# The first layer's experts computed for two chosen experts per token, in 39 gathered tiles, instead of for all eight

## The reference, cut to what matters

```python
xn = _layernorm(x)
x = x + _L0_attn_ref(xn, wq, wk, wv, wa, wg, wo, rms_scale) + _L0_ffn_ref(xn, wqkv, w1, w2)

# attention: a complex gate, a scan over the 512 tokens of a sequence
a_c = sigmoid(|a|) * exp(i * angle(a));  y = q * real(scan(a_c, k * v));  return (y * silu(g)) @ wo

# experts: E = 8, F = 352, the best TOP_K = 2 of a token
top_logits, idx = lax.top_k(logits, 2);  scores = softmax(top_logits)
for e in range(8):
    a, g = split(x_rep @ w1[e].T)              # 128 -> 2 * 352
    he = silu(a) * g @ w2[e].T                 # 352 -> 128
    out = out + where(expert_ids == e, he, 0)
out = (out * scores).reshape(N, 2, h).sum(axis=1)
```

## Time and profile before

| | us |
|---|---|
| median of 3 runs | 523.91 (523.36 to 526.57) |
| profiled execution | 524.22 |
| its span, first to last instruction | 522.4 |
| head, until the first attention matmul | 44.3 |
| each of the first three turns of the loop | 64.5 |
| fourth turn, until the last 12 token tiles' statistics begin | 59.9 (237.8 to 297.7) |
| until the first normalised token tile of layer two (L895) | 304.92 |
| second layer | 217.5 |

### The profile page before, as it was taken

How to read it: one execution, slowest core, us unless ns; L and a number is a source line. 1 busy time by engine, 2 the same in 40 slices (tenths; PEclk the granted TensorE clock), 3 DMA queues, 4 the chain that set the end, 5 groups by cost and what they waited for, 6 DMA issues and landing times.

```text
span 522.4 us, 7319 instructions
## 1 busy us (share of the span) xinstructions
PE 442.2 (85%) x2143; PEld 325.9 (62%) x2143; DVE 382.8 (73%) x702; ACT 278.1 (53%) x392; POOL 194.8 (37%) x188
## 2 busy tenths in 40 slices
PE   2729999999999999999989969299689778977893
PEld 1327887888878888788877845155455445544452
DVE  5687478944888448894498987776768877887784
ACT  2375674426644275533655255835676577557730
POOL 1248014400144001530002100740477778777850
PEclk9958999999999999999999979579799999999997
DMA  6420001100012000000000000000265776687664
GB/s 177 96 61 23 2 0 43 43 1 0 0 41 52 0 0 0 0 0 0 1 0 2 1 0 1 0 2 0 55 130 114 144 141 131 116 157 137 126 130 120
DMA packets 29535, 26.76 MB, mean 51 GB/s; under 512 B 10837, under 2 KB 25414, under 8 KB 29510
## 3 DMA queue, kind: packets, MB, share of 16 engines
q0 software_dynamic: 4608, 16.78, 16.8%
q1 hardware_dynamic: 24902, 9.69, 7.3%
HBM read 8.64 MB, written 1.05 MB: 19 GB/s over the span
## 4 chain that ended last, share of the span: by engine, by line
PE 29%; DVE 28%; POOL 19%; issue 13%; ACT 7%; DMA 2%; DVEq 1%; SPq 0%; POOLq 0%; ACTq 0%
POOL state L435 9%; PE psum L1083 7%; PE psum L203 6%; PE psum L205 6%; PE psum L204 6%; POOL xn_tok L439 4%; POOL g_hi L448 3%; DVE hid L771 2%; PE psum L1203 2%; DVE at_m L800 1%; DVE at_m L802 1%; POOL g_lo L449 1%; DVE xn_tok L693 1%; POOL sel_now L450 1%; PE psum L1218 1%
## 5 line engine op out<-in xcount | busy, mean ns | idle before, releaser
L567 ACT ACTIVATE sil<-psum 128x512 f32<-128x512 f32 (+1 forms) x96 | 56.3, 596 | 104.3 <-PE psum L205 91.2
L771 DVE TENSOR_TENSOR hid<-sil,psum 128x512 f32<-128x512 f32 (+1 forms) x96 | 65.1, 686 | 51.8 <-PE psum L205 32.9
L1083 PEld LDWEIGHTS psum<-e_w,hid 128*128 128x128 f32 (+1 forms) x768 | 94.9, 191 | 6.0
L1083 PE MATMUL psum<-e_w,hid 128*128 128x128 f32 (+1 forms) x768 | 95.3, 274 | 0.0
L203 PE MATMUL psum<-xn_hi,e_hi 128*128 128x512 f32 (+1 forms) x192 | 81.8, 426 | 7.9 <-DVE hid L771 7.3
L975 DVE TENSOR_TENSOR_SCAN state<-dec,win_t 128x1024 f32<-128x1024 f32 x32 | 73.4, 2295 | 20.0 <-ACT dec L643 20.0
L205 PE MATMUL psum<-xn_lo,e_hi 128*128 128x512 f32 (+1 forms) x192 | 76.0, 396 | 0.0
L204 PE MATMUL psum<-xn_hi,e_lo 128*128 128x512 f32 (+1 forms) x192 | 75.8, 395 | 0.0
L652 ACT ACTIVATE sil<-psum,vec_t 128x512 f32<-128x512 f32 x64 | 43.2, 687 | 47.3 <-PE psum L205 36.8
L435 POOL TENSOR_SCALAR state<-state,ssm_cb 128x1024 f32<-128x1024 f32 x32 | 49.7, 1552 | 45.2 <-DVE state L975 42.2
L1258 PE MATMUL psum<-hid,g_w 128*128 128x512 f32 x128 | 61.3, 592 | 0.0
(11 more groups left out here) (261 smaller groups left out, 766.5 us busy)
## 6 DMA issues: line engine op xcount, KB each, us to landing
xn_tok<-state POOLq DMA_DIRECT2D x32, 512.0 KB, 4.5
e_raw<-in_L_ffn_w SPq DMA_DIRECT2D x16, 128.0 KB, 2.1
e_raw<-in_L_ffn_w SPq DMA_DIRECT2D x8, 176.0 KB, 2.4
res<-in_L_attn_x SPq DMA_DIRECT2D x4, 256.0 KB, 3.9
g_raw<-in_L_ffn_w SPq DMA_DIRECT2D x16, 64.0 KB, 2.3
g_w<-in_L_ffn_w SPq DMA_DIRECT2D x16, 64.0 KB, 2.5
out<-res SPq DMA_DIRECT2D x4, 256.0 KB, 2.9
e_raw<-in_L_ffn_w SPq DMA_DIRECT2D x16, 48.0 KB, 1.9
```

What stands on the lines that cost most here:

```text
L567: act.activation(sil[0:M, s % 2, :], ps[s % 2][0:M, :], ACT.Silu).then_inc(silu_done, 1)
L771: dve.tensor_tensor(hid[0:M, tb % 2, ft, :], sil[0:M, s % 2, :], ps[2 + s % 2][0:M, :], ALU.mult).then_inc(gated, 1)
L1083: ins = pe.matmul(ps[4 + o % 2][:, n * P:(n + 1) * P], hid[0:m, tb % 2, ft, n * P:(n + 1) * P], e_w2[j][0:m, ft, :], start=(ft == 0), stop ...
```

## The change

**What it does.** All eight experts' weights are turned, copied and split before the first layer's main part, and stay in SBUF (`w_hi`, `w_lo`, `w_out`). After the mask `chosen`, PE counts with two matmuls how many tokens chose each expert, and some thirty small DVE instructions give every (token, choice) pair a slot in a table of 39 tiles of 128 slots, each tile of one expert; 39 is the 32 tiles that 4096 pairs fill, plus 7 for rounding up. SP fills the table `slots` in HBM with zeros; POOL writes the 2048 tokens twice to it, by 32 indirect DMAs of 128 rows. A row is 130 numbers: the token, its weight, its place in the output.

**Tiles.** SP loads a tile of slots (`x_tile`, a ring of six); from the seventh on it waits until the output of the tile six before has landed. Per tile PE turns it (`turn_x`), makes 2 x 352 hidden channels with six matmuls (`hidden`), turns them (`turn_hidden`) and multiplies with w2 (`output`). The number of the tile's expert is read by PE from SBUF into a register (`value_load`), for `hidden` and again for `output`. ACT copies, applies Silu, copies and weighs (`copy_x`, `tile_silu`, `copy_hidden`, `weigh_out`); DVE splits and gates (`split_x`, `gate`); POOL scatters the 128 output rows to `parts` in HBM by an indirect DMA (`send`, three buffers). After the last tile SP loads `parts` back as two rows per token (`both`), DVE adds both to `res`, and all statistics follow.

**Attention.** Its instructions are the same. Of its 100 steps (4 blocks of 25) 58 stand ahead of the tiles: blocks 0 and 1, and steps 0 to 7 of block 2. The other 42 are spread behind the 39 tiles, one to two per tile.

```diff
+        AHEAD_STEPS = 58
+        att_steps = [(i, s) for i in range(NB) for s in range(STEPS + 1)]
+
+        def beside(n):
+
+            left = len(att_steps) - AHEAD_STEPS
+            done = [AHEAD_STEPS + left * m // NTILE for m in (n, n + 1)]
+            return att_steps[done[0]:done[1]]
...
+            for e in range(2, E0):
+                sp.wait_ge(e_turned, 2 * (e - 2) + 2)
+                load_expert(e, e % 2)
+            sp.wait_ge(fill_ready, 1)
+            sp.dma_start(slots.rearrange("(n p) r -> p n r", p=P),
+                         fill[:, None, :].to_broadcast([P, NTILE, ROW])).then_inc(slots_filled, 16)
...
-            with sp.Fori(0, NB - 1) as i:
-                for j in range(EPI):
-
-                    sp.wait_ge(e_turned, i * 2 * EPI + 2 * j + 2)
-                    load_expert(i * EPI + EPI + j, j)
+            sp.wait_ge(scattered, 16 * NT * TOPK)
+            for n in range(NTILE):
+                if n >= XRING:
+                    sp.wait_ge(o_sent[(n - XRING) % ORING], 16 * ((n - XRING) // ORING + 1))
+                sp.dma_start(x_tile[n % XRING][:, :], slots[n * P:(n + 1) * P, :]).then_inc(x_tile_in[n % XRING], 16)
+            sp.wait_ge(att_pe, NB * N_ATT_PE)
+            for r in range(ORING):
+                sp.wait_ge(o_sent[r], 16 * ((NTILE - 1 - r) // ORING + 1))
+            parts_v = parts[NTILE * P:NTILE * P + NTOK * TOPK, :].rearrange("(c p k) d -> p c (k d)", p=P, k=TOPK)
+            for b in range(NB):
+                sp.dma_start(both[:, b * TPB:(b + 1) * TPB, :, :].rearrange("p c k d -> p c (k d)"),
+                             parts_v[:, b * TPB:(b + 1) * TPB, :]).then_inc(both_in[b], 16)
...
+                    pool.nop().then_inc(pads_ready, 1)
+
+            pool.wait_ge(slots_ready, 1)
+            pool.wait_ge(slots_filled, 16)
+            for t in range(NT):
+                for k in range(TOPK):
+                    pool.indirect_dma_start(
+                        out=slots, out_offset=bass.IndirectOffsetOnAxis(ap=to_slot[k][:, t:t + 1], axis=0),
+                        in_=rows[k][:, t, :], in_offset=None).then_inc(scattered, 16)
...
+            def send(n):
+
+                pool.wait_ge(o_out, n + 1)
+                pool.wait_ge(part_ready, n + 1)
+                pool.indirect_dma_start(
+                    out=parts, out_offset=bass.IndirectOffsetOnAxis(ap=part[:, n:n + 1], axis=0),
+                    in_=t_out[n % ORING][:, :], in_offset=None).then_inc(o_sent[n % ORING], 16)
+
+            for i, s in att_steps[:AHEAD_STEPS]:
+                attention(i, s)
+            for n in range(-2, NTILE + 2):
+                if n >= 2:
+                    send(n - 2)
+                if 0 <= n < NTILE:
+                    for i, s in beside(n):
+                        attention(i, s)
 
...
+            def weigh_out(n):
+
+                act.wait_ge(o_made, n + 1)
+                if n >= ORING:
+                    act.wait_ge(o_sent[n % ORING], 16 * (n // ORING))
+                act.activation(t_out[n % ORING][:, :], ps[O_BANK][:, 0:P], ACT.Copy,
+                               scale=x_tile[n % XRING][:, D:D + 1]).then_inc(o_out, 1)
...
+            def split_x(n):
+
+                dve.wait_ge(x_hi_ready, n + 1)
+                dve.tensor_tensor(xt_lo[n % 2][:, :], ps[X_BANK][:, 0:P], xt_hi[n % 2][:, :].bitcast(F32),
+                                  ALU.subtract).then_inc(x_lo_ready, 1)
+                dve.tensor_tensor(part[:, n:n + 1], x_tile[n % XRING][:, D + 1:D + 2], spare[:, n:n + 1], ALU.max
+                                  ).then_inc(part_ready, 1)
...
+            dve.wait_ge(att_dve, NB * N_ATT_DVE + 1)
+            for b in range(NBLK):
+                dve.wait_ge(both_in[b], 16)
+                r = res[:, b * TPB:(b + 1) * TPB, :]
+                for k in range(TOPK):
+                    own(dve.tensor_tensor(r, r, both[:, b * TPB:(b + 1) * TPB, k, :], ALU.add))
...
+            def expert_of(n):
+                return bass.ds(pe.value_load(tile_e[0:1, n:n + 1], min_val=0, max_val=E0 - 1), 1)
+
+            def turn_x(n):
+
+                pe.wait_ge(x_tile_in[n % XRING], 16 * (n // XRING + 1))
+                if n >= 1:
+                    pe.wait_ge(x_lo_ready, n)
...
+            def hidden(n):
+
+                e = expert_of(n)
+                pe.wait_ge(x_lo_ready, n + 1)
+                if n >= 1:
+                    pe.wait_ge(gated, n)
+                half = [slice(0, F), slice(F, F2)]
+                acc = [ps[A_BANK][:, 0:F], ps[G_BANK][:, 0:F]]
+                for c in range(2):
+                    pe.matmul(acc[c], xt_hi[n % 2][:, :], w_hi[:, e, half[c]].rearrange("p a f -> p (a f)"),
+                              start=True, stop=False)
+                for c in range(2):
+                    pe.matmul(acc[c], xt_hi[n % 2][:, :], w_lo[:, e, half[c]].rearrange("p a f -> p (a f)"),
+                              start=False, stop=False)
+                for c in range(2):
+                    ins = pe.matmul(acc[c], xt_lo[n % 2][:, :], w_hi[:, e, half[c]].rearrange("p a f -> p (a f)"),
+                                    start=False, stop=True)
+                ins.then_inc(h0_made, 1)
...
+            def output(n):
+
+                e = expert_of(n)
+                pe.wait_ge(h_copied, n + 1)
+                if n >= 1:
...
+                    ins = pe.matmul(ps[O_BANK][:, 0:P], t_hid_t[n % 2][:, c * P:(c + 1) * P],
+                                    w_out[:, e, c, :].rearrange("p a d -> p (a d)"),
+                                    start=(c == 0), stop=(c == NF - 1))
+                ins.then_inc(o_made, 1)
...
+            for n in range(-2, NTILE + 2):
+                if 0 <= n < NTILE:
+                    hidden(n)
+                if n + 2 < NTILE:
+                    turn_x(n + 2)
+                if 0 <= n - 1 < NTILE:
+                    turn_hidden(n - 1)
+                if n >= 2:
+                    output(n - 2)
+                if 0 <= n < NTILE:
+                    for i, s in beside(n):
+                        attention(i, s)
 
```

More of the change, by code:

```diff
@@ L120, in program @@
         pair = sb("pair", [P, NT, E0 * E0])
+        base = here()
         pair2 = sb("pair2", [P, NT, E0 * E0])
+        proj_raw = over(base, nc.sbuf_base)("proj_raw", [P, 6, P])
         rsm = sb("rsm", [P, 4, NT, E0])
@@ new lines, in program @@
+        staged = over(base, nc.sbuf_base)
+        e_raw1 = [staged(f"e_raw1_{j}", [P, 2 * NF, P]) for j in range(2)]
+        e_raw2 = [staged(f"e_raw2_{j}", [P, F]) for j in range(2)]
+        e_t = [staged(f"e_t_{j}", [P, F2]) for j in range(2)]
+        base = here()
+        w_hi = sb("w_hi", [P, E0, F2], F32R)
+        w_lo = sb("w_lo", [P, E0, F2], F32R)
+        w_out = sb("w_out", [P, E0, NF, P])
+        later = over(base, nc.sbuf_base)
+        DECS = 3
+        dec = [later(f"dec_{j}", [P, NTOK]) for j in range(DECS)]
@@ L154, in program @@
+        state = [later(f"state_{k}", [P, NTOK // 2]) for k in range(4)]
+        hid = later("hid", [P, 2, NF, TB])
+        sil = later("sil", [P, 2, TB])
+        base = here()
         dt_t = sb("dt_t", [P, NTOK])
@@ L365, in _, with attend, attention @@
                 split_group(j)
[L367 to L376 removed]
+            def attend(out, a, b, op):
+                pool.tensor_tensor(out, a, b, op).then_inc(att_pool, 1)
+            def attention(i, s):
@@ L774, in turn, with flat @@
-            def turn(i, last):
-                att = Chain(dve, att_dve, i * N_ATT_DVE + 1)
+            dve.wait_ge(ranked, 1)
+            before, total = (ps[0][:, n * P:(n + 1) * P].rearrange("p (t e) -> p e t", e=E0) for n in range(2))
+            n_e, tiles, upto_tiles, shift, prior = (per_e[:, n, :] for n in range(5))
+            last, whole, second, unused = (per_t[:, n, :] for n in range(4))
+            def flat(a):
+                return a[:, :, :].rearrange("p e t -> p (e t)")
+            own(dve.tensor_copy(place[:, :, :], total))
@@ L874, in turn @@
-                if not last:
-                    gate(i + 1, 0)
-                attention(STEPS)
-                if not last:
-                    gate(i + 1, 1)
-                add_output(OUTS - 1)
-                assert att.n == N_ATT_DVE
-            for s in range(2):
-                gate(0, s)
-            with dve.Fori(0, NB - 1) as i:
-                turn(i, False)
-            turn(NB - 1, True)
-            dve.wait_ge(o_added, NB * OUTS + 2)
+                if s == 2:
+                    pe_step(1)
+                    act_step(1)
+                    att(dve.tensor_tensor(A["kv"], ps[7][:, :], A["k"], ALU.mult))
@@ L1134, in attention @@
                     dve_step(24)
-                    if not last:
-                        pe.wait_ge(e_copied, copied + 3)
                     for n in range(TPB):
```

656 lines of the change are left out of this document (333 added, 323 removed).

## The result

The changed kernel takes **579.93 us** (median of 4 runs, 577.21 to 583.29) against 523.93 us (4 runs): ratio **1.106**, 95% interval 1.1005 to 1.1124. Its profiled execution has a span of 581.5 us, the one before 522.4: 59.1 us more. The first layer carries nearly all of it. The normalization ahead of the second layer, at 304.92 before, now starts at 362.54, 57.6 later; from there to the end are 219.0 us, before 217.5.

A forecast was written before the change was run, and what follows sets the result against it. The first layer was taken as bound by PE's matmuls, which the change removes, exposing attention. 66 + 88 + 29 + 195 + 18 = 396 us against 304.9, 91 more, so 615 us; 20% lay outside 540 to 695.

The forecast's parts named there:

- the forecast's own case: Whole kernel: tiles take 4 to 5.5 us a pass, giving 590 to 655 us; chance 55%.
- 1. first projection at: Head: six more experts' preparation, counting and slots make attention start at 66 us, not 44.3; bounds 63 and 69.
- 2. attention ahead: Attention ahead of the tiles: exposed chains, 40 us a block plus 8 for block 2's first steps, 88 us.
- 3. POOL late for block 0: Attention block 0 waits for POOL behind 32 scatters at 1.2 us each: 29 us late, between 10 and 61.
- 4. tiles, first turn to last weighing: Expert tiles: PE and the ring hand over to each other, 4.6 us a pass, 195 us in all.
- 5. between the layers: After the last weighing: landing, loading both, adds and statistics before the second layer, 18 us.
- The rule of the Trainium skill: POOL-issued DMAs beside busy DVE take about five times as long; not followed, placed within the 22% rival at 710 us.
- The ring of loads: Tiles: tile n + 6 loads once tile n has landed; a turn of 8.9 us over two passes, 4.45 each.
- The other limit: Tiles: PE's matmuls at 3.1 us plus two reads of tile_e at 0.8 each, 4.7 us per tile.
- Cheap handovers: Rival, 15%: reads 0.2 or less, indirect issue 0.6 to 0.9; 3.4 to 3.6 a pass; 548, up to 575 us.
- Dear ones: Rival, 22%: reads 1.5 to 2 or issue 2 and more; 6 to 7 a pass, POOL 50 late; 650 to 760 us.
- The other side: Rival, 8%: faster or same, tiles hide under attention at 2.5 us a pass; 502 us.

The follow-up runs named there:

- e1_spread: Against the change: POOL's order only, scatter cut in four groups, sel ahead of the wait for slots, second layer's splits behind the tiles; 553.82 us.
- e8_sel_late: Against e6: ring of 12 loads, one read of tile_e per tile, and the work on sel moved behind the last tile; 525.00 us.
- e5_ahead100: Against the change: all 100 attention steps ahead of the tiles instead of 58, none beside them; 637.04 us.
- e2_ring12: Against the change: ring of token tiles (XRING) 12 instead of 6; 560.97 us.
- e6: Against e1_spread, keeping its POOL order: 33 attention steps ahead of the tiles instead of 58; 533.53 us.
- e9: Against e8_sel_late: attention's pieces among the tiles placed by a table of passes for each engine; 533.90 us.
- e12: Against e9: five of attention's ACT functions become Copy, so results are not the reference's; 511.97 us.
- e11: Against e8_sel_late: five of attention's ACT functions become Copy, so results are not the reference's; 516.20 us.

## Why the prediction was right, and where it was not

The direction was right, and so was the reason: the kernel is slower because chains that PE's work had hidden now stand in the open, and because POOL's queue makes block 0 late. PE's busy time in the first layer fell by 95 us, not by "far more than 100", at a clock of 0.72 and no longer 0.98. The time, 580, is 35 under the forecast of 615, and 10 below the 590 at which the forecast's own case began; one term accounts for that.

| step | forecast | measured |
|---|---|---|
| 1. first projection at | 66 | 66.08 |
| 2. attention ahead | 88 | 90.7 (121.0 less the next row) |
| 3. POOL late for block 0 | 29 | 30.3 (wait of 31.5, in block 1 of 1.2) |
| 4. tiles, first turn to last weighing | 195 | 157.4 |
| 5. between the layers | 18 | 18.1 |
| normalization starts | 396 | 362.5 |

**1. Head.** Right in sum and in most of its parts: the counting at 53.9 (54.5, though the parts given add up to 54.1), slots at 61.4 (61.5). One step was wrong: the fill takes 17.1 us from issue, not 14, and lands just before POOL's first DMA at 63.0, not by 60. POOL waited for it last, 1.6 us beyond the slots. That does not show in this term, but it stands in POOL's lateness below.

**2. Attention.** From block 0's last add to block 1's are 41.5 us, forecast 40 as a pure chain.

**3. POOL.** I took 1.2 per indirect DMA; it is 0.97 and 0.30 between two, 1.27. That the size fitted is partly luck. The reason given, that it would be dearer in itself than the direct one of 0.89, was only a small part: the direct DMA's row does not contain the time ahead of it, which the trace of before has as well, 0.30 at each. e1_spread shows that nearly the whole wait stood on the path: it takes the wait away, and the first tile comes 25.3 us earlier behind a head that is 4.8 longer. The rule of the Trainium skill in SBUF — State Buffer, SBUF: two separate sides, would have made it some 90 us: that did not come. In the 32 DMAs the longest has 1447 ns, and all that lie above the median come to 1.3 us together. One of the longer ones, at 88.05 above, starts while DVE's scan runs (87.40 to 88.63). This is a weak test of the rule, though: DVE is busy 13.5 of the first 25.6 us of the scatter and stands idle in the last 16, waiting for POOL. The same section says that a VectorE instruction in a two-port mode, or one with two inputs in SBUF beside a GpSimd instruction that reads there, and a GpSimd instruction exclude each other: whichever starts first keeps the shared pair to its end. This case's traces agree in the other direction, with POOL first: e1_spread's scan and copy lose 3.2 us in the head, e8_sel_late gives them back, and some 4 us are lost between the layers when the same work is moved there. I had weighed the rule for DMAs only.

**4. Tiles: the term that was mis-sized.** 4.6 a pass was forecast; it is 3.4 for the tiles alone (e5_ahead100) and 3.9 with attention's pieces. The ring of loads with two passes a turn is a limit, as forecast, and e2_ring12 removes its waits. But I counted 8.9 for a turn and it is 6.9. The link from the weighed output to the next tile in SBUF takes 4.4, not 5.8: I put POOL's issue (1.2) ahead of the landing (1.9), while a send lands 2.26 after its start, issue included; and the load takes 1.86, not the 2.4 read from loads in a group. PE's and ACT's part takes 2.5, not 3.1, and more than half of that difference is the read of `tile_e`: 302 ns and its two register instructions 169 more, 0.47 and not 0.8. The Trainium skill's floor of 0.6 for such a load (DMA: Bandwidth & Descriptors, Latency and other measured facts) does not hold here: the trace has half of it.

The other limit, PE at 4.7 a pass, the larger of the two in the forecast, was wrong: with the ring of 12, passes with both reads take 2.5 to 2.8. The reads have 0.94 of that and not 1.6, and the matmuls some 1.8 at a clock of 1.00, where I had put 3.1 by a clock of 0.76 from a stretch with PE half busy. The mean clock in the tiles was 0.87, with 0.95 from 202 to 250.

In the other direction, attention's pieces among the tiles cost 19.6 us and not 10: I had counted ACT's lumps only, while in the tiles of the change (187 to 345) attention's own waits of DVE, 8.7 and 5.1 us for ACT and 4.1 for POOL, stand in the same queue as the next tile's gate. What each engine's share of the 19.6 is was not measured. So 1.2 us a pass too much over 38 passes, 46 in all, stand against 10 too little for the pieces: that the term is off by 38 only, and the time by 35, is in part luck. The six fast passes of about 3 also make 18 and not the 15 in the sum.

**5. Between the layers.** Right in sum: landing 2.23, not 3, `both` 3.89, not 3, then 11.5 (11.8).

**The rivals.** "Cheap handovers" described the passes best (3.4 to 3.6; 3.4 measured for the tiles alone), but POOL was as late as in the forecast, not 10 to 20. The result lies in the gap between that rival (up to 575) and the forecast's own case (from 590), which I gave no chance of its own. "Dear ones" did not occur. The other side needed 2.5 a pass and attention's cost hidden. 2.5 to 2.8 is what single passes reach once the ring is larger. With less attention ahead (e6 to e8) the kernel comes level with the one before but not below it: attention then sets half of the passes.

## What to carry to other kernels

When the engine that bounds a kernel loses its work, add up the chains that it had hidden, and ask of every in-order queue what new work stands ahead of an old step; that gave four of five terms within 3 us. A ring's turn is to be read from issue to landing and to use, once, and not built from rows that overlap. If work is to hide beside short passes, look at its largest piece per pass on any engine, table loads with it, and not at its mean; and try the order with the largest pieces taken out, since a better order can look worse while they stand.

## What the runs showed of the hardware

- An indirect DMA of 128 rows takes POOL 0.96 or 0.97 us in most runs (32 scatters and 39 sends each; median 1.00 and 1.14 for the sends of e9 and e12), and 0.30 us pass before the next. The longest send has 1.04 with no attention beside the tiles (e5_ahead100), 1.89 in the change. Sends of 64 KB land 2.2 to 2.4 after their start in the median.
- A register read from SBUF on PE's queue takes 302 ns (78 reads), with the two register instructions behind it 0.47.
- While POOL's affine_select on 128x2048 in bfloat16 runs (2.43 us each), DVE's scan of 128x128 takes 1.69 instead of 0.42 and a copy of 128x7 2.10 instead of 0.17; two adds of 128x512 take 5.55 instead of 1.39.
- A table load of ACT takes 1.283 us each time, 13 of them beside the tiles in e8_sel_late.
- Filling 2535 KB of HBM from a 128x130 tile in SBUF by one DMA takes 17.1 us from issue to landing.

What stays open: how much the table of passes would give with the product for wo one pass later, what the passes would be with neither ring nor attention beside them, and which version beats the kernel before with the whole computation. Of the runs that keep it none does, and e8_sel_late comes nearest; e11 and e12, at 0.986 and 0.978 of the time before, have Copy in place of attention's functions.
